# Layer 0's routed gate and up as three products of split operands, the halves made one block ahead

## The reference

```python
logits = jnp.einsum('th,eh->te', xt.astype(jnp.float32), w_router.astype(jnp.float32))
scores = jax.nn.sigmoid(logits)
topk_w, topk_i = jax.lax.top_k(scores, TOPK)
...
gate = jax.nn.silu(jnp.einsum('th,eih->tei', xt, wg))
up = jnp.einsum('th,eih->tei', xt, wu)
expert_out = jnp.einsum('tei,ehi->teh', gate * up, wd)
out = jnp.einsum('te,teh->th', comb, expert_out)
```

## Time and profile before

| | before |
|---|---|
| median of 3 runs | 1029.61 us (1023.4 to 1030.06) |
| profiled execution, its own time | 1035.81 us |
| its span, first to last instruction | 1034.0 us |
| mean granted PE clock | 0.872 of full |
| PE / DVE / ACT busy, share of the span | 75% / 56% / 31% |
| routed blocks' loop | from about 298 to about 484 us of the span |

### The profile page before, as it was taken

The page is one execution under the profiler, slowest core; times in us unless marked ns, Lnnn a source line. Parts: engine busy times, 40 slices in busy tenths (PEclk is TensorE's granted clock), DMA queues, the critical chain, the costliest instruction groups (busy, mean ns, idle before and its releaser), DMA issues. The chain is left out here.

```text
span 1034.0 us, 13203 instructions
## 1 busy us (share of the span) xinstructions
PE 773.6 (75%) x4289; PEld 486.1 (47%) x4291; DVE 576.0 (56%) x1369; ACT 318.6 (31%) x730; POOL 243.4 (24%) x295
## 2 busy tenths in 40 slices
PE   3576667399999998997034689988898818999990
PEld 1334343178856665555012355555555404565550
DVE  2767866634422222222355689999996553454544
ACT  1222222143322222221012366566665411122220
POOL 1102111150000000001613323445553321232332
PEclk9888787589999999999555699999999858999995
DMA  9150522056107787673340000101104118899936
GB/s 345 80 203 2 203 97 108 27 177 232 59 5 259 274 305 284 236 269 109 97 161 6 0 1 21 36 30 44 43 25 150 38 41 309 267 342 316 316 138 218
DMA packets 52691, 151.90 MB, mean 147 GB/s; under 512 B 6705, under 2 KB 36273, under 8 KB 47377
## 3 DMA queue, kind: packets, MB, share of 16 engines
q1 hardware_dynamic: 47296, 135.99, 37.3%
q0 software_dynamic: 5328, 15.08, 3.9%
HBM read 109.87 MB, written 41.17 MB: 146 GB/s over the span
## 5 line engine op out<-in xcount | busy, mean ns | idle before, releaser
L1144 PE MATMUL ps<-f_rw,f_xT 128*128 128x512 f32 (+1 forms) x276 | 114.2, 538 | 12.3 <-DMA f_rw<-w_routed 11.7
L1058 DVE TENSOR_TENSOR f_rh<-f_gate,ps 128x256 f32<-128x256 f32 (+1 forms) x69 | 26.0, 377 | 138.9 <-ACT f_gate L1004 85.8
L1923 ACT ACTIVATE b_PX<-ps 128x512 f32<-128x512 f32 x128 | 72.7, 597 | 42.6 <-PE ps L2139 40.6
L1670 DVE TENSOR_REDUCE b_smax<-ps 128x4 f32<-128x1024 f32 x64 | 77.6, 1213 | 13.0 <-PE ps L2115 12.8
L959 POOL DMA_INDIRECT f_yg<-y,dest x16 | 15.2, 949 | 266.3 <-DMA y<-f_ys 261.8
L1144 PEld LDWEIGHTS ps<-f_rw,f_xT 128*128 128x128 f32 x276 | 51.6, 192 | 45.1 <-issue 24.1
L2368 POOL DMA_INDIRECT y<-f_ys,f_to x47 | 45.1, 959 | 115.1 <-DVE f_ys L2417 113.6
L1004 ACT ACTIVATE f_gate<-ps 128x256 f32<-128x256 f32 (+1 forms) x69 | 24.0, 348 | 139.4 <-PE ps L1144 138.9
L1165 PE MATMUL ps<-f_rw,f_rhT 128*128 128x256 f32 x230 | 61.1, 381 | 0.4 <-DVE f_ys L1050 0.4
L2139 PE MATMUL ps<-b_Q,b_Cx 100*128 100x256 f32 x256 | 54.7, 319 | 6.2 <-ACT b_PX L1923 5.7
L2115 PE MATMUL ps<-b_Cx,b_Q 96*128 96x512 f32 x128 | 46.8, 449 | 11.8 <-ACT b_Q L1907 6.3
(11 more groups left out here) (322 smaller groups left out, 1768.2 us busy)
## 6 DMA issues: line engine op xcount, KB each, us to landing
f_rw<-w_routed SPq DMA_DIRECT2D x23, 1920.0 KB, 7.9
rows<-a_blank SPq DMA_DIRECT2D x16, 1152.0 KB, 9.3
rw<-w_ffn SPq DMA_DIRECT2D x24, 704.0 KB, 5.8
f_rw<-w_ffn SPq DMA_DIRECT2D x23, 704.0 KB, 5.8
f_xs<-rows SPq DMA_DIRECT2D x47, 144.0 KB, 5.0
f_yk<-y SPq DMA_DIRECT2D x8, 512.0 KB, 7.7
f_raw<-w_shared SPq DMA_DIRECT2D x10, 384.0 KB, 3.9
b_Cx<-ctx_parts SPq DMA_DIRECT2D x96, 32.0 KB
```

The source lines that it names most:

```text
L1058: nc.vector.tensor_tensor(rh[u % 2][:, 0:n], gate[u % 2][:, 0:n], ps[:, u % 4, n:2 * n], ALU.mult).then_inc(r_h, 1)
L1144: mm = nc.tensor.matmul(ps[:, u % 4, 0:2 * n], xT[b % 2][:, c, :], rw[b % R_SLOTS][:, off:off + 2 * n], start=(c == 0), stop=(c == C - 1))
L1670: nc.vector.tensor_reduce(smax[t % 2][:, k // C, k % C, :], ps[:, FIRST:FIRST + 2, :].rearrange("p u (g n) -> p (u g) n", g=2), AX, ALU.ma ...
L1923: nc.scalar.activation(PX[g % RING][:].rearrange("p c m -> p (c m)"), ps[:, RETS + G_TURN[g] % 2, :], ACT.Exp, scale=XSC).then_inc(turn_re ...
```

## The change

Routed gate and up become three float32r products per half c, as in the shared experts. For that the gate and up weights of every block are split by ACT (`high_w`) and DVE (`low_w`) unit by unit into two buffers each, `rw_hi` and `rw_lo`, one block ahead: the split of unit u + 3 stands in both loops ahead of unit u's own work. The rows are split as well, while being copied out of PSUM (`high_x` on ACT, `keep_x` on DVE). PE waits for the low half of its unit in place of the load. The new buffers reuse the space of the shared experts' halves. Down products, the three weight buffers and SP's program stay.

```diff
+            def high_w(u):
+                b, (at, n) = u // PER, PARTS[u % PER]
+                if u % PER == 0:
+                    act.wait_ge(rw_loaded[b % R_SLOTS], 16 * (b // R_SLOTS + 1))
+                    if b >= 2:
+                        act.wait_ge(r_scored, PER * (b - 1))
+                part = rw[b % R_SLOTS][:, 0:RD].rearrange("p (c n) -> p c n", c=C)[:, :, 2 * at:2 * at + 2 * n]
+                high = rw_hi[b % 2].rearrange("p (c n) -> p c n", c=C)[:, :, 2 * at:2 * at + 2 * n]
+                nc.scalar.copy(high, part).then_inc(rw_high, 1)
+
+            def high_x(b):
+                act.wait_ge(x_turned, b + 1)
+                if b >= 2:
+                    act.wait_ge(r_scored, (b - 1) * PER)
+                nc.scalar.copy(xT_hi[b % 2][:].rearrange("p c t -> p (c t)"), ps[:, 6, 0:D]).then_inc(x_high, 1)
+
+            act.wait_ge(oT_dve, HALVES)
+            high_x(0)
+            for u in range(PER):
+                high_w(u)
             for u in range(RU):
+                if u + PER < RU:
+                    high_w(u + PER)
                 n = PARTS[u % PER][1]
                 act.wait_ge(r_scored, u + 1)
                 if u >= 2:
                     act.wait_ge(r_h, u - 1)
                 nc.scalar.activation(gate[u % 2][:, 0:n], ps[:, u % 4, 0:n], ACT.Silu).then_inc(r_silu, 1)
+                if u % PER == 0 and u // PER + 1 < BLOCKS0:
+                    high_x(u // PER + 1)
                 if u >= T_LAG:
                     keep_hT(u - T_LAG)
...
             def keep_x(b):
-                dve.wait_ge(x_turned, b + 1)
-                if b >= 2:
-                    dve.wait_ge(r_scored, (b - 1) * PER)
-                nc.vector.tensor_copy(xT[b % 2][:].rearrange("p c t -> p (c t)"), ps[:, 6, 0:D]).then_inc(x_kept, 1)
+                dve.wait_ge(x_high, b + 1)
+                nc.vector.tensor_tensor(xT_lo[b % 2][:].rearrange("p c t -> p (c t)"), ps[:, 6, 0:D],
+                                        xT_hi[b % 2][:].bitcast(F32).rearrange("p c t -> p (c t)"), ALU.subtract).then_inc(x_kept, 1)
+
+            def low_w(u):
+                b, (at, n) = u // PER, PARTS[u % PER]
+                dve.wait_ge(rw_high, u + 1)
...
+                nc.vector.tensor_tensor(low, part, high.bitcast(F32), ALU.subtract).then_inc(rw_low, 1)
...
             keep_x(0)
+            for u in range(PER):
+                low_w(u)
             for u in range(RU):
+                if u + PER < RU:
+                    low_w(u + PER)
                 b, i, n = u // PER, u % PER, PARTS[u % PER][1]
                 dve.wait_ge(r_silu, u + 1)
...
                 if i == 0:
-                    pe.wait_ge(rw_loaded[b % R_SLOTS], 16 * (b // R_SLOTS + 1))
                     pe.wait_ge(x_kept, b + 1)
+                pe.wait_ge(rw_low, u + 1)
                 if u >= 4:
                     pe.wait_ge(r_h, u - 3)
                 for c in range(C):
                     off = c * 2 * I0 + 2 * at
-                    mm = nc.tensor.matmul(ps[:, u % 4, 0:2 * n], xT[b % 2][:, c, :], rw[b % R_SLOTS][:, off:off + 2 * n],
-                                          start=(c == 0), stop=(c == C - 1))
+                    mm = three(ps[:, u % 4, 0:2 * n], xT_hi[b % 2][:, c, :], xT_lo[b % 2][:, c, :], rw_hi[b % 2][:, off:off + 2 * n],
+                               rw_lo[b % 2][:, off:off + 2 * n], c == 0, c == C - 1)
                 mm.then_inc(r_scored, 1)
```

More of the change, by code:

```diff
@@ L857, in routed_experts @@
         raw = [sb(f"raw{n}", [P, WC]) for n in range(W_SLOTS)]
-        wh = [sb(f"wh{n}", [P, WC], F32R) for n in range(W_SLOTS)]
-        wl = [sb(f"wl{n}", [P, WC], F32R) for n in range(W_SLOTS)]
+        split_bufs = sb("split_bufs", [P, 2 * W_SLOTS * WC + 2 * H_SLOTS * HT], F32R)
+        wh = [split_bufs[:, n * WC:(n + 1) * WC] for n in range(W_SLOTS)]
+        wl = [split_bufs[:, (W_SLOTS + n) * WC:(W_SLOTS + n + 1) * WC] for n in range(W_SLOTS)]
+        HB = 2 * W_SLOTS * WC
         act_out = [sb(f"act{n}", [P, HT]) for n in range(2)]
         h = [sb(f"h{n}", [P, HT]) for n in range(H_SLOTS)]
-        hh = [sb(f"hh{n}", [P, HT], F32R) for n in range(H_SLOTS)]
-        hl = [sb(f"hl{n}", [P, HT], F32R) for n in range(H_SLOTS)]
+        hh = [split_bufs[:, HB + n * HT:HB + (n + 1) * HT] for n in range(H_SLOTS)]
+        hl = [split_bufs[:, HB + (H_SLOTS + n) * HT:HB + (H_SLOTS + n + 1) * HT] for n in range(H_SLOTS)]
         zeros = sb("zeros", [P, HT], BF16)
@@ L868, in routed_experts @@
         xs = [sb(f"xs{n}", [P, D]) for n in range(X_SLOTS)]
-        xT = [sb(f"xT{n}", [P, C, P]) for n in range(2)]
+        rw_hi = [split_bufs[:, n * RD:(n + 1) * RD] for n in range(2)]
+        rw_lo = [split_bufs[:, (2 + n) * RD:(3 + n) * RD] for n in range(2)]
+        xT_hi = [sb(f"xT_hi{n}", [P, C, P], F32R) for n in range(2)]
+        xT_lo = [sb(f"xT_lo{n}", [P, C, P], F32R) for n in range(2)]
         gate = [sb(f"gate{n}", [P, 256]) for n in range(2)]
@@ L895, in routed_experts @@
         x_turned = sem("x_turned")
+        x_high = sem("x_high")
         x_kept = sem("x_kept")
+        rw_high = sem("rw_high")
+        rw_low = sem("rw_low")
         r_scored = sem("r_scored")
@@ L1040, in keep_x @@
             def keep_x(b):
-                dve.wait_ge(x_turned, b + 1)
-                if b >= 2:
-                    dve.wait_ge(r_scored, (b - 1) * PER)
-                nc.vector.tensor_copy(xT[b % 2][:].rearrange("p c t -> p (c t)"), ps[:, 6, 0:D]).then_inc(x_kept, 1)
+                dve.wait_ge(x_high, b + 1)
[4 more added lines that the diff above has]
+                dve.wait_ge(rw_high, u + 1)
+                part = rw[b % R_SLOTS][:, 0:RD].rearrange("p (c n) -> p c n", c=C)[:, :, 2 * at:2 * at + 2 * n]
+                high = rw_hi[b % 2].rearrange("p (c n) -> p c n", c=C)[:, :, 2 * at:2 * at + 2 * n]
+                low = rw_lo[b % 2].rearrange("p (c n) -> p c n", c=C)[:, :, 2 * at:2 * at + 2 * n]
+                nc.vector.tensor_tensor(low, part, high.bitcast(F32), ALU.subtract).then_inc(rw_low, 1)
             def keep_y(b):
```

## The result

The change makes the kernel slower: 1152.5 us (median of 4 runs, 1148.9 to 1155.4) against 1028.1 (the median of 4 runs of the kernel before), a ratio of 1.122, 95% interval 1.116 to 1.127. The profiled execution spans 1149.3 us.

What follows compares the result with a forecast made beforehand. Weight load (7.5 us) and ACT/PE work to the next issue (6.3) run in series: 13.8 us a period against 8.04. 19 periods +109, start +0.5, end +4.1: +114 on the median 1029.6, forecast 1143 us, range 1102 to 1162.

Steps and rivals of the forecast that it cites:

- The wait that moves: ACT's cast for block b+1 waits for a load just issued, holding up the copy PE needs; about 7 us each.
- the ring: Routed loop: weight load and the ACT and PE work up to the next load's issue run in series, 13.8 us a period.
- The chain: ACT and PE work from a load's landing to the next load's issue: 6.3 us with PE partly at half speed.
- full clock: Rival: same closed loop of load and work, PE stays at 2.4 GHz; period 12.0 us, +77, 1106 us; chance 0.20.
- The load: A routed block's weight load from issue to landing, taken as 7.5 us with only one under way.
- the sum: Added time: start +0.5, 19 periods +109, from load 22's issue to the last copy +4.1; total +114 us.
- The clock: PE's pause of about 5.5 us a block drops it to half speed, making the period 13.8 us, not 12.0.
- Half clock: PE at 1.2 GHz until 5.6 us after each load's landing; period 13.8 us, chance 0.62.
- Start and end: Load 3 issued 0.5 us later; from load 22's issue to the last block's copy 22.9 us, +4.1.
- Signs: Expected in the profile: 20 cast waits of about 7 us, DMA share about 0.45, loop end at 595 to 600 us.
- The split is really hidden: Rival: weights have landed when ACT needs them, so only PE's saving counts; 1022 us, at best 1012; chance 0.07.
- PE's 0.8: PE's saving per block from float32r gate and up products: 3.5 us against 4.28.

Runs made afterwards that it cites:

- e7: Kernel before with one wait added: ACT waits for block b+1's load at the head of block b's turn, no casts; 1.102 of the kernel before.
- e1: Changed kernel with the cast and subtraction of unit u+3 moved to the end of unit u's turn, behind the copy; 1.052 of the kernel before.
- e5: Changed kernel with each weight load split into a gate and up transfer and a down transfer, three buffers each; 0.971 of the kernel before.
- e9: Changed kernel with four weight buffers in place of three, still one transfer a block; 0.976 of the kernel before.
- e3: Changed kernel with 40 added float32r products a block from block 3 on, where PE would wait for ACT's copy; 1.090 of the kernel before.
- e8: Changed kernel with all three casts and subtractions of the next block at the very end of a block's turn; 1.050 of the kernel before.
- e2: Changed kernel with all three casts and subtractions of block b+1 behind the copy of (b-1, 2); 1.033 of the kernel before.
- e10: Changed kernel with split gate and up and down transfers, but two gate and up buffers in place of three; 0.988 of the kernel before.

## Why the prediction was right

The mechanism was the forecast one at every step. The forecast was +114 us; the loop has +122.1. In time it was 1143 us with a range of 1102 to 1162, and 1152.5 was measured. Of the 8.1 us that the loop has more, the load has about 6, the chain 1.6 and the start 0.8.

- **The wait that moves.** 20 casts wait on the load and 20 downs on the copy, as stated. e7 shows that the place of the wait is enough, e1 that the ring's length follows from what stands behind it, e5 that with more lead it is gone, and e9 that with one turn more what is left of it, some 2 us a block, hardly reaches PE. ACT comes to its wait 0.2 us ahead of the load's issue (439.97 and 440.18), not some tenths behind it as forecast.
- **The chain.** Forecast from landing to issue 6.3 us at half clock; over 19 periods it is 14.18 less the mean load of 7.8, 6.4. In the period shown: 1.9 to PE's start (forecast 1.9), 3.15 for down and gate and up (3.16), 0.42 for the turn (0.42), 1.24 for the last down and the issue (0.8 forecast, since full clock was to be back by then; in other periods it was: casts at 577.67, issue at 583.61, 5.9).
- **The load.** Taken as 7.5, measured 7.8 on average (7.4 to 8.2). 0.3 x 19 = 6 us, the largest error of the sum. The estimate of 6.5 us by the Trainium skill's "DMA: Bandwidth & Descriptors", "Anatomy of one DMA", which is for a DMA issued by GpSimd, is 1.3 a load below the measured 7.8, 25 us over 19 periods; the measurement decides.
- **The clock.** Half clock was the forecast, and the 13.8 us that hangs on it were 14.18; full clock would have been 12.0, and e3, which has it, shows 12.63. e3 puts its price at 33 us of the 124. PE's own busy time says it too: it was to fall by 18 us, and rose by 17. By the Trainium skill's rule that long DMA waits between matmuls let the array go cold ("TensorE: Matmul & The Clock Gate", "Loop structure matters more than you think") it was to be half clock too; the trace agrees: behind each of the 20 pauses, 5.1 to 6.1 us long, the four down records took 2.07 or 2.08 us, and the clock was 0.84 on average from 380 to 460 us.
- **Start and end.** Forecast +0.5 and +4.1, measured +1.3 and +4.0.
- **Signs.** The loop ends at 606.8 us, not at 595 to 600, and ACT's casts wait 8.2 us, not 7; the first follows from the sum's 8.1 us, the second from the longer load and from ACT's arrival ahead of the issue. The DMA share of 0.45 and the 20 waits came as stated.
- **Rivals.** "The split is really hidden" did not happen in this kernel; e5 and e9 are what it takes. Its price was set too low at 7 us, or 18 at best with no limit from the loads: 30 us in e5 (2.9%), since there the waits for loads went as well as PE's 0.8.

## What to carry to other kernels

A wait put into an in-order queue is paid by all that stands behind it. Before placing one, follow what stands behind it to the instruction that frees the buffer which the awaited load's successor needs; if the path closes, load and chain add up and no slack hides them. Work done "one block ahead" needs its input loaded one block earlier, that is one buffer more or a buffer freed sooner, and this must come with the change. A free buffer is not enough: in e10 the load stood behind other issues in SP's queue when its buffer was free.

## What the runs showed of the hardware that I had not expected

- PE fell to half clock behind 16 of 19 pauses of 2.28 us in e8. In the kernel before, 12 of the 13 pauses, up to 1.64 us, left it at full clock, and the one of 2.05 us did not the earlier trace rows (the window from 380 to 400 has two of them, not one as the prediction says); in e2 one of 3.02 us left it there (1.00 from 482 to 488 us). So in these runs the length of a single pause did not settle it.
- Filling a wait with 5.0 us of useless products a block made the changed kernel 3% faster (e3).
- A float32r product that follows float32 ones shows a start too early by 0.19 us and a longer record (0.58 for 0.40, as at 442.35 to 442.77), yet the sum of both is as before: 441.67 to 442.77 is 1.10 = 0.87 + 0.23. So I take it for the way the record is drawn, not for time.
